# Two-layer block, one core: the gathered rows of the second layer's experts get sixteen buffers, are summed in place, and six result tiles move behind the last shared batch

## The reference, cut to what matters

```
shared = silu_and_mul(x @ shared_gate_up_w.T) @ shared_down_w.T      # 704 hidden features
shared = shared * sigmoid(x @ sgate_w.T)
topk_w, topk_ids = top_k(softmax(x @ gate_w.T), 4)                   # 16 experts, 4 for each token
for e: acc += (silu_and_mul(x @ w13[e].T) @ w2[e].T) * coef_e
g = shared + acc                                                     # then x + s * silu(g)
```

## Time and profile before

| | |
|---|---|
| median of three runs | 1173.21 us (1172.02 to 1177.78) |
| the profiled execution, its own time | 1177.82 us |
| its span | 1176.0 us |
| PE, DVE, ACT, POOL busy | 86%, 72%, 56%, 46% of the span |
| mean granted clock of PE | 0.94 |
| POOL's 64 gathers | first issued at 1055.2 us, last at 1161.2 us |

### The profile page before, as it was taken

How to read it: one execution, slowest core, us unless ns; L and a number is a source line. 1 busy time by engine, 2 the same in 40 slices (tenths; PEclk the granted TensorE clock), 3 DMA queues, 4 the chain that set the end, 5 groups by cost and what they waited for, 6 DMA issues and landing times.

```text
span 1176.0 us, 22134 instructions
## 1 busy us (share of the span) xinstructions
PE 1014.1 (86%) x6741; PEld 660.4 (56%) x6741; DVE 846.6 (72%) x2231; ACT 662.6 (56%) x1720; POOL 541.0 (46%) x532
## 2 busy tenths in 40 slices
PE   4966788855789999899999999999888899997775
PEld 2544533324355676676666666767645688863333
DVE  4576546765588869868678999999847877764466
ACT  1533334433567865967866567666537777762222
POOL 0468455520465466543444345444321455525563
PEclk9979898986899999999999999999989999998897
DMA  9867399849465367031111100210167455543232
GB/s 340 303 193 295 83 305 318 258 187 330 79 131 125 96 118 156 20 90 37 59 51 37 37 24 14 86 37 1 62 194 213 115 144 146 144 104 101 81 99 90
DMA packets 96959, 155.99 MB, mean 133 GB/s; under 512 B 12208, under 2 KB 67248, under 8 KB 94032
## 3 DMA queue, kind: packets, MB, share of 16 engines
q1 hardware_dynamic: 77120, 115.42, 30.0%
q0 software_dynamic: 19728, 39.21, 15.3%
HBM read 104.84 MB, written 45.02 MB: 127 GB/s over the span
## 4 chain that ended last, share of the span: by engine, by line
PE 54%; DVE 16%; ACT 9%; issue 8%; DVEq 4%; POOL 3%; DMA 2%; POOLq 1%; another core or an unknown queue 1%; ACTq 1%; SPq 0%
PE ps L1071 8%; PE ps L1240 6%; PE ps L1134 5%; PE ps L1084 5%; PE ps L1122 4%; PE ps L1102 3%; PE ps L886 3%; PE ps L1203 2%; ACT arena L1488 2%; PE ps L1186 2%; PE ps L1258 2%; PE ps L968 2%; DVE arena L2213 1%; PE ps L1230 1%; PE ps L985 1%
## 5 line engine op out<-in xcount | busy, mean ns | idle before, releaser
L2300 POOL TENSOR_TENSOR arena<-arena 128x512 f32<-128x512 f32 x128 | 174.7, 1424 | 112.3 <-ACT arena L1465 112.3
L1071 PE MATMUL ps<-arena 128*128 128x512 f16 x768 | 177.5, 381 | 1.3 <-ACT arena L1465 1.3
L2305 POOL TENSOR_TENSOR arena<-arena 128x512 f32<-128x512 f32 x64 | 66.6, 1041 | 178.0 <-DVE arena L1954 178.0
L2342 POOL DMA_INDIRECT wvo<-xn_d,idx x79 | 75.9, 961 | 116.8 <-PE ps L1230 97.1
L1071 PEld LDWEIGHTS ps<-arena 128*128 128x128 f16 x768 | 75.0, 98 | 93.3 <-ACT arena L1465 3.5
L1488 ACT ACTIVATE arena<-arena 128x128 f32<-128x128 f32 x256 | 99.2, 390 | 41.6 <-DVEq L1949 41.5
L1464 ACT ACTIVATE arena<-ps 64x512 f32<-64x512 f32 x128 | 76.1, 595 | 53.6 <-DVE arena L1922 49.4
L1134 PE MATMUL ps<-wvo,arena 128*128 128x256 f16 x768 | 96.5, 278 | 5.7 <-DVE s_sb L1974 2.9
L1084 PE MATMUL ps<-wvo,arena 128*128 128x512 f16 x384 | 94.4, 382 | 5.6 <-ACT arena L1474 2.7
L1922 DVE TENSOR_TENSOR arena<-ps,wvo 128x512 f32<-128x512 f32 x128 | 84.8, 684 | 19.3 <-PE ps L1071 18.7
L1122 PE MATMUL ps<-arena 128*128 128x192 f32 (+1 forms) x512 | 94.8, 329 | 2.4 <-DVE arena L1960 2.4
(11 more groups left out here) (292 smaller groups left out, 2235.9 us busy)
## 6 DMA issues: line engine op xcount, KB each, us to landing
arena<-wqk_d SPq DMA_DIRECT2D x16, 1024.0 KB, 5.5
arena<-in_wgu SPq DMA_DIRECT2D x32, 384.0 KB
y_d<-wvo SPq DMA_DIRECT2D x79, 128.0 KB
z_d<-wvo SPq DMA_DIRECT2D x8, 1024.0 KB, 4.2
z_d<-wvo SPq DMA_DIRECT2D x2, 4096.0 KB, 27.4
arena<-in_wdn SPq DMA_DIRECT2D x32, 192.0 KB
arena<-z_d SPq DMA_DIRECT2D x12, 512.0 KB, 4.6
arena<-z_d POOLq DMA_DIRECT2D x12, 512.0 KB
```

What stands on the lines that cost most here:

```text
L1071: last = pe.matmul(ps[s][:, :], wqk[gg][:, s * DC + c, w, hh * DH:(hh + 1) * DH], hx[bb][:, :, x, c * P:(c + 1) * P], start=(c == 0 and w ...
L2300: nc.gpsimd.tensor_tensor(qk_s[:, s], qk_s[:, s], sin, ALU.mult).then_inc(sin_done, 1)
```

## The change

`yr` gets a buffer for each of the 16 tiles, in the tensor `arena` over the routed experts' weights, which nobody reads any more by then. So `gather_choices` no longer waits for `sum_done`: POOL issues all 64 gathers in a row. `mix1`, the sum, is no tensor of its own but the first of the tile's four gathered rows, so the sum is made in place. The shared part `sh` of tiles 4 to 15 moves into `wvo`, over the buffers from which the routed results were stored; ACT waits for those stores before it writes the first of them. Each tile needs a count of its own for its gathers: `rows_landed` takes semaphores that earlier stages used and have done with. Last, `RESULT_AT` is another table, and six tiles (10 to 15) instead of four stand behind the last step; their `out_gate` stands behind all four `shared_out` of the last batch and no longer between them.

```
-        yr = wv_flat.rearrange("p (u k d) -> p u k d", u=4, k=K1)
+        yr = arena[:, 0:NT * K1 * D].rearrange("p (n k d) -> p n k d", n=NT, k=K1)
...
-        mix1 = arena[:, 0:NT * D].rearrange("p (n d) -> p n d", n=NT)
+        mix1 = yr[:, :, 0]
+        assert NT * K1 * D <= at_sgw
...
-        sh = arena[:, NT * D:(2 * NT - TPB) * D].rearrange("p (n d) -> p n d", n=NT - TPB)
+        sh = wv_flat[:, 0:(NT - TPB) * D].rearrange("p (n d) -> p n d", n=NT - TPB)
+        rows_landed = [(s, 0) for s in yr_in] + [(s, 16 * PAIRS // XGBUF) for s in gathered[4:]]
+        rows_landed += [(s, Z_ADDED + 16 * ADDS * (NB - 1)) for s in z_added]
+        rows_landed += [(gathered[u], 16 * PAIRS // XGBUF + 16 * ((XT - u + 3) // 4)) for u in range(4)]
...
-        RESULT_AT = {(1, 5): (0, 1, 2), (2, 1): (3,), (2, 3): (4,), (2, 5): (5, 6, 7), (3, 1): (8,), (3, 2): (9,), (3, 3): (10,), (3, 5): (11,)}
-        LAST_BATCH = range(NT - TPB, NT)
+        RESULT_AT = {(1, 5): (0, 1), (2, 1): (2,), (2, 2): (3,), (2, 4): (4,), (2, 5): (5,), (3, 1): (6, 7), (3, 3): (8,), (3, 5): (9,)}
+        LAST_TILES = range(10, NT)
...
+                if b == 1:
+                    for u in range(4):
+                        act.wait_ge(y1_out[u], 16 * ((XT - u + 3) // 4))
                 for k in range(TPB):
                     for t in RESULT_AT.get((b, FC - 1), ())[k:k + 1]:
                         out_gate(t)
                     shared_out(TPB * b + k)
-                    if b == NB - 1:
-                        out_gate(TPB * b + k)
+            for t in LAST_TILES:
+                out_gate(t)
...
-                u = t % 4
-                dve.wait_ge(yr_in[u], 16 * K1 * (t // 4 + 1))
+                landed, before = rows_landed[t]
+                dve.wait_ge(landed, before + 16 * K1)
...
             def gather_choices(t):
-                seen(pool, sum_done, t - 4)
                 for j in range(K1):
```

More of the change, by code:

```diff
@@ L544, in build @@
         sh0 = wo_flat[:, 12 * D + 2 * F1:16 * D + 2 * F1].rearrange("p (n d) -> p n d", n=TPB)
-        sh = arena[:, NT * D:(2 * NT - TPB) * D].rearrange("p (n d) -> p n d", n=NT - TPB)
+        sh = wv_flat[:, 0:(NT - TPB) * D].rearrange("p (n d) -> p n d", n=NT - TPB)
+        rows_landed = [(s, 0) for s in yr_in] + [(s, 16 * PAIRS // XGBUF) for s in gathered[4:]]
+        rows_landed += [(s, Z_ADDED + 16 * ADDS * (NB - 1)) for s in z_added]
+        rows_landed += [(gathered[u], 16 * PAIRS // XGBUF + 16 * ((XT - u + 3) // 4)) for u in range(4)]
+        assert len(rows_landed) == NT
         block = ctx.enter_context(nc.Block())
@@ L2212, in result_sum @@
                 for j in range(K1):
-                    last = nc.vector.scalar_tensor_tensor(mix1[:, t], yr[:, u, j], w4[:, t, j:j + 1], part, ALU.mult, ALU.add)
+                    last = nc.vector.scalar_tensor_tensor(mix1[:, t], yr[:, t, j], w4[:, t, j:j + 1], part, ALU.mult, ALU.add)
                     if j < K1 - 1:
@@ L2233, in _ @@
                             result(t - 1)
-            for t in LAST_BATCH:
+            for t in LAST_TILES:
                 result_sum(t)
@@ L2344, in gather_choices @@
             def gather_choices(t):
-                seen(pool, sum_done, t - 4)
                 for j in range(K1):
-                    pool.indirect_dma_start(yr[:, t % 4, j], None, y1_d,
-                                            bass.IndirectOffsetOnAxis(ap=row1[:, t * K1 + j:t * K1 + j + 1], axis=0)).then_inc(yr_in[t % 4], 16)
+                    pool.indirect_dma_start(yr[:, t, j], None, y1_d,
+                                            bass.IndirectOffsetOnAxis(ap=row1[:, t * K1 + j:t * K1 + j + 1], axis=0)).then_inc(rows_landed[t][0], 16)
             for j in range(XT):
```

## The result

| | median us | lowest to highest | ratio to before, 95% interval |
|---|---|---|---|
| before (4 runs) | 1175.2 | 1172.0 to 1177.8 | |
| changed (4 runs) | 1232.7 | 1231.8 to 1240.8 | 1.051 [1.0475, 1.0542] |

A fourth execution has moved the median of before from 1173.2 to 1175.2.

A forecast was written before the change was run, and what follows sets the result against it. The path was taken to go PE, ACT, DVE and back for each step, then a tail of DVE sums. Tail 7.2, batch 2 3.1 and late hand-overs 4 sum to 14.3 on 1173.2: 1187 us, range 1181 to 1193.

The forecast's parts named there:

- the late hand-overs: Batches 2 and 3: ACT takes PE's ended products late while gathers run unbroken; +4 us, bounds 0 and 12.5.
- the first two stay: Fifth and sixth products, up to about 1075 us: both kernels alike there, so these late hand-overs remain unchanged.
- the 7.5 for three pairs: Steps (2, 1) to (3, 0): three pairs of steps handed over late cost between 0 and 7.5 us.
- Buffers, waits and places: Sixteen buffers, in-place sums, ACT's wait for stores and the waits on a tile's own gathers: each costs 0.
- POOL waits, and nobody waits for POOL: After the routed experts: POOL's 26.7 us of waits hold up no sum, so more buffers gain nothing by themselves.
- Tail: From the last `shared_lo` to the end: 28.1 us against 20.9, +7.2; lower bound +4.5, upper bound 7.2.
- Batch 2: Between steps (2, 1) and (2, 5): three tiles stand where two did, +3.1 us, bounds 0 and 3.1.
- batch 3: Between product (3, 1) and the end of (3, 5): three tiles before and after, two now together, cost 0.
- The first: Rival: every hand-over is late while gathers run, 22.8 us slower, 1196 us; chance 0.18.
- The second: Rival: late hand-overs of batches 2 and 3 go away, giving back 15.6 us, 1165 us; chance 0.09.
- The third: Rival: gathers were on the path ahead of the sums, at most 2.8 us come back, 1170 us; chance 0.04.
- the fourth: Rival: nine sums instead of eleven ahead of the last step give back 5.8 us, 1178 us; chance 0.13.

The follow-up runs named there:

- e2: Changed kernel with the old order of sums, results and out gates, keeping sixteen buffers, in-place sums and unbroken gathers: 1221.4 us, ratio 1.040.
- e3: Changed kernel with one wait added, the four gathers of tile t waiting for the sum of tile t-4: 1176.2 us, ratio 1.004.
- e1: Kernel before with the new order of sums, results and out gates, keeping its own four shared buffers: 1181.3 us, ratio 1.007.
- e12: Kernel before with one memset of 128x256 on GpSimd ahead of each gather, nothing else changed: 1161.5 us, ratio 0.9855.
- e11: Changed kernel with the old order of sums and results and one memset of 128x256 ahead of each gather: 1158.4 us, ratio 0.983.
- e13: Changed kernel with eight memsets of 128x256 ahead of each two tiles' gathers, so close runs of eight: 1152.3 us, ratio 1.007.
- e15: Changed kernel with each gather fetching half a row, 512 bytes for each of 128 partitions, no pacing: 1154.1 us, ratio 1.009.
- e16: Changed kernel with the old order of sums and results and four memsets of 128x256 ahead of each tile's four gathers: 1155.0 us, ratio 1.011.
- e9: Changed kernel with one memset of 128x128 on GpSimd ahead of each gather, gathers 1.34 us apart: 1231.1 us, ratio 1.046.
- e17: The changed kernel itself, run once more, where the kernel before took 1173.2 us: 1231.0 us, ratio 1.051.
- e10: Changed kernel with four memsets of 128x256 ahead of each tile's four gathers and none between these: 1161.3 us, ratio 0.988.

## Why the prediction was wrong

*Failed step: the late hand-overs, "I take +4", with bounds of 0 and 12.5.* Late hand-overs inside a run of gathers were named, and their place and direction were right; the term measured 49.2 us (e2 against before). The upper bound was no bound. It priced each late hand-over at 8.4 us, as though the wait were the same however old the run of gathers is, and 8.4 wasn't even the longest: the sixth product, ended by 1067.88, was taken at 1077.92, 10.0 us late. All of these came in runs of at most twenty us, and the text said so; the waits grow with the run (1.7, 8.6, 28.8, 31.7 us). And two of those of before were over soon after their run of gathers was: the sixth product came 3.0 us behind the end of the last gather at 1074.94, the one of 1100.22 came 2.1 us behind the end of this one, the last before a pause of 8.2 us:

```profile
1097.15 0.94 POOL L2347 DMA_INDIRECT wvo<-y_d,row  x1 [0.30 <-issue]
```

So "the first two stay" failed too: with the run unbroken the sixth product came at 1104.09. The rows of before hinted at it: none late in a run's first steps, 5 and 6 us late towards its end. A wait that depends on a length isn't bounded by rows at shorter lengths. A slip beside it: the 7.5 for three pairs counts the one with two tiles at 2.5, though by the same text it takes 10.2 anyway and 9.6 doesn't lengthen it; 5.0 was meant.

*Buffers, waits and places: 0.* Right for what was priced: e3 has all of them, and the new order, at 1.004. But "POOL waits, and nobody waits for POOL" was read as if those 26.7 us were worth nothing. Without them the kernel took 49 us more.

*Tail: +7.2, lower bound 4.5.* Measured +4.4 (25.3 against 20.9), the lower bound, for the reason it gave: PE ran those matmuls in 8.76 us, and DVE waited 1.8 us where 4.5 were forecast. *Batch 2: +3.1.* The spacing of 5.12 us is there. *Both with batch 3, 10.3 in sum:* e1 has the order alone at 9.1, with an interval of 4 to 12 us, and e3 has order and buffers at 4.0.

*Rivals.* The first, every hand-over late (1196 us), was the nearest in kind; its price was the same false bound. The second, faster because late hand-overs vanish, is wrong for this change; that its 15.6 us for those of batches 2 and 3 lie near the 14.6 for all in e12 is luck. The third (gathers on the path, 2.8 us) isn't settled: e3 keeps the gathers' waits, and e11 and e12, with sixteen buffers and four, differ by 3.1 us within their intervals. Of the fourth (two tiles fewer pay, +4.5 us for the order) the interval of e1 doesn't decide; e3 speaks for it and e13 to e15, 9 to 11 us slower without a stall, against it.

*What would show it.* The 64 gathers took 80.0 us as forecast and ended at 1132.6, having begun 2.5 us sooner. ACT's waits stood in the place named, but were up to 31.7 us where "5 us or more" was written. The three signs of being wrong (last `shared_lo` before 1150, hand-overs on time, a tail near 21 us) all stayed away: they guarded against a faster result only.

## What to carry to other kernels

An idle engine's pause can be what lets another engine run: before removing a wait that nobody waits for, look at what will be unbroken without it. Where GpSimd issues many gathers in a row and TensorE works beside them, look for idle time of PE ended by "issue" and products taken late, and put the gathers a little further apart or into runs of four; 0.33 us of idle work for each turned 1.05 into 0.99 here. It isn't free: where the chip showed no stall, the paced kernel with the old order (e16) was 1% slower than the kernel before. A bound taken from short stretches doesn't hold for a long one, and a time should be tried on more than one chip.

## What was not expected of the hardware

- Long runs of indirect gathers from GpSimd (128 rows of 1 KB) 1.25 or 1.34 us apart held up TensorE's work; 1.44 us apart they didn't, and 64 plain DMAs of the same size in 34 us didn't either (on a chip where the close gathers weren't tried).
- The gathers' transfers kept pace all the while, in the ten microseconds from 1085 with 106 GB/s and no other engine at work; 128 KB in 1.25 us is 105. So the transfers didn't fall behind the issue. The windows of the changed kernel (busy us of PE, PEld, DVE, ACT and POOL, granted clock, DMA share, GB/s):

```profile
1050.00:1150.00 100.00, 37.89 (x156) 16.95 (x154) 13.71 (x24) 9.98 (x18) 60.77 (x64) 0.63 0.32 92
1055.00:1065.00 10.00, 10.00 (x48) 4.46 (x46) 4.60 (x8) 4.31 (x7) 7.70 (x8) 1.00 0.37 104
1085.00:1095.00 10.00, 0.00 (x0) 0.00 (x0) 0.00 (x0) 0.00 (x0) 7.56 (x9) 0.50 0.36 106
```

- The granted clock was 1.00 from 1055 to 1065, when the fourth product came late and PE worked on the next two, and 0.50, the lower level, once PE had stood still. So it didn't cause the stall.
- Chips differ: those of e2, e9 and e17 had the stall; that of e13 to e16 showed none in the kernels it ran, and ran the kernel before in 1143.5 us against 1172 to 1176 on the four others. Not all of these 30 us lie in the gathers' stretch: the first gather came at 1044.9 in e16 and at 1051.1 in e10, which have the same pacing.

Open are: what GpSimd's indirect issue and PE share, and whether it is the indirect issue or the scattered addresses; whether the bytes of a row count (e15 ran only on the chip without a stall); whether the changed kernel stalls on that chip; the bound between runs of four and sixteen; and whether the stall is there when no trace is taken, since every execution here was recorded.
